# Relative attention on one core: two masked queries and the first products moved ahead, diagonals waited for block by block

## What is computed

```python
qx, kx, vx = split_head(x @ Wq.T), split_head(x @ Wk.T), split_head(x @ Wv.T)
ex = rel_embed[ns].reshape(n, NH, HD).transpose(1, 0, 2)
srel = srel_skew(jnp.einsum('bhnd,hmd->bhnm', qx, ex))
qk = (jnp.einsum('bhnd,bhmd->bhnm', qx, kx) + srel) * inv_dim
atten = jax.nn.softmax(qk - mask, axis=-1)
out = jnp.einsum('bhnm,bhmd->bhnd', atten, vx).transpose(0, 2, 1, 3).reshape(b, n, d)
return out @ Wp.T + bp
```

## Time and profile before

| | |
|---|---|
| median of three runs | 3797.18 us (3792.64 to 3798.52) |
| the profiled execution | 3799.16 us, of which the span of instructions 3797.1 us |
| PE busy | 3561.5 us, 94% |
| PEld, DVE, ACT, POOL busy | 63%, 60%, 46%, 22% |
| granted clock of TensorE, mean | 0.992 |

### The profile page before, as it was taken

How to read it: one execution, slowest core, us unless ns; L and a number is a source line. 1 busy time by engine, 2 the same in 40 slices (tenths; PEclk the granted TensorE clock), 3 DMA queues, 4 the chain that set the end, 5 groups by cost and what they waited for, 6 DMA issues and landing times.

```text
span 3797.1 us, 78536 instructions
## 1 busy us (share of the span) xinstructions
PE 3561.5 (94%) x31023; PEld 2402.4 (63%) x31023; DVE 2288.1 (60%) x7482; ACT 1731.8 (46%) x3542; POOL 822.9 (22%) x1374
## 2 busy tenths in 40 slices
PE   6999999988999999998899999998889999999888
PEld 3666667666565667766556556776665656677665
DVE  4546455677554655567755554567776555456766
ACT  2425333466442523356644252335565335233556
POOL 3202023411210302332021030333302112033330
PEclk8999999999999999999999999999999999999999
DMA  3000000000000000000000000000000000000000
GB/s 89 2 1 2 1 1 1 2 2 2 13 1 1 2 1 1 1 2 2 1 13 1 1 2 1 1 1 2 2 7 8 1 1 1 1 1 1 2 2 9
DMA packets 27032, 17.47 MB, mean 5 GB/s; under 512 B 9425, under 2 KB 26274, under 8 KB 26658
## 3 DMA queue, kind: packets, MB, share of 16 engines
q1 hardware_dynamic: 26658, 12.32, 1.2%
HBM read 10.22 MB, written 2.10 MB: 3 GB/s over the span
## 4 chain that ended last, share of the span: by engine, by line
PE 69%; DVE 11%; POOL 7%; ACT 6%; issue 5%; SPq 1%; DVEq 0%; another core or an unknown queue 0%; POOLq 0%
PE banks L1252 9%; PE banks L1219 8%; PE banks L1214 8%; PE banks L1064 5%; PE banks L1103 5%; POOL work L563 5%; PE banks L1118 4%; PE banks L1043 3%; PE banks L1306 3%; PE banks L1538 3%; ACT work L887 2%; ACT work L881 2%; PE banks L1373 2%; PE banks L1551 2%; DVE work L2034 2%
## 5 line engine op out<-in xcount | busy, mean ns | idle before, releaser
L1723 DVE CUSTOM_DVE_ANT_0 work<-banks,mask_row 128x512 f32<-128x512 f32 (+3 forms) x1024 | 433.9, 486 | 276.1 <-PE banks L1064 276.0
L718 ACT ACTIVATE work<-banks 128x512 f32<-128x512 f32 x352 | 209.3, 597 | 654.1 <-PE banks L1214 638.9
L1814 DVE TENSOR_TENSOR work<-work,banks 128x512 f32<-128x512 f32 x352 | 242.0, 688 | 426.5 <-PE banks L1219 404.6
L519 POOL TENSOR_TENSOR rstd<-rstd,half 128x4 f32<-128x4 f32 x65 | 65.6, 1009 | 1933.9 <-DVE rstd L1647 1933.9
L741 ACT ACTIVATE work<-banks 128x384 f32<-128x384 f32 (+1 forms) x768 | 358.8, 534 | 255.2 <-PE banks L1103 254.7
L1103 PE MATMUL banks<-work 32*128 32x512 f32 (+3 forms) x2048 | 443.8, 464 | 6.5 <-DVE work L1723 3.9
L1252 PEld LDWEIGHTS banks<-wd,work 128*128 128x128 f32 (+2 forms) x4096 | 355.0, 189 | 135.3 <-issue 131.4
L1064 PE MATMUL banks<-work 32*128 32x384 f32 (+3 forms) x2048 | 406.1, 457 | 11.9 <-ACT work L727 6.4
L1252 PE MATMUL banks<-wd,work 128*128 128x128 f32 (+2 forms) x4096 | 365.8, 278 | 0.0
L530 POOL TENSOR_SCALAR_AFFINE_SELECT work<-work 128x128 f32<-128x128 f32 (+1 forms) x768 | 253.4, 333 | 460.8 <-ACT work L741 437.5
L1103 PEld LDWEIGHTS banks<-work 32*128 32x128 f32 x2048 | 243.0, 183 | 77.2 <-ACT work L741 39.4
(11 more groups left out here) (320 smaller groups left out, 6596.6 us busy)
## 6 DMA issues: line engine op xcount, KB each, us to landing
x_a<-in_L_attn_a_x_dram SPq DMA_DIRECT2D x5, 256.0 KB, 2.8
x_b<-in_L_attn_a_x_dram SPq DMA_DIRECT2D x4, 256.0 KB, 3.0
wg<-in_L_ffn_Wg_dram SPq DMA_DIRECT2D x2, 512.0 KB
wu<-in_L_ffn_Wu_dram SPq DMA_DIRECT2D x2, 512.0 KB
wd<-in_L_ffn_Wd_dram SPq DMA_DIRECT2D x16, 64.0 KB
out_dram<-x_a SPq DMA_DIRECT2D x4, 256.0 KB, 2.5
out_dram<-x_b SPq DMA_DIRECT2D x4, 256.0 KB, 2.6
wk_l<-in_L_attn_a_Wk_dram SPq DMA_DIRECT2D x1, 512.0 KB, 4.1
```

Of the source, the lines that this page charges most:

```text
L1723: m = eng.tensor_tensor_reduce(out=summed[:, k % 2, col:col + N], in0=bank(bk)[:, col:col + N], in1=mask_row[:, T - N:T], scale=1.0, scala ...
```

## The change

Five edits, all in the relative attention.

1. The float32 rest of q goes to the buffer of normalized rows (`xns`), that of k to the memory of the second masked-query buffer. The first masked-query buffer is free from the start of the call.
2. DVE's order is new: the rest of q, masked high part for c = 0, the rest of k, masked middle part for c = 0, low part of q, low part of k, values, then c = 1, then both copies of spread k. Before it was: both rests, both low parts, values, both masks of c = 0, the first copy of spread k, c = 1, the second copy.
3. POOL's masked part for c = 1 waits for DVE's two masks of c = 0 (`r_qm`) in place of the low parts.
4. PE runs group 0 of the products first; the wait for the values and the spread steps 0 and 1 come between groups 0 and 1.
5. DVE's wait for all 32 diagonal instructions is split over the first three adds: job 0 waits for 29, job 1 for 31, job 2 for all.

```diff
--- before.py
+++ after.py
@@ -206,8 +206,9 @@
         q_st, at = part(0, [H // 2, T], BF16)
         k_st, at = part(at, [H // 2, T], BF16)
         ring_at = at
-        res, at = part(ring_at, [2, T])
-        k_parts, at = part(at, [3, T], BF16)
+        k_parts, _ = part(ring_at + 2 * T, [3, T], BF16)
+        res_k, _ = part(ring_at + 2 * T + 3 * T // 2, [T])
+        at = ring_at + 2 * T + 3 * T // 2
         q_parts, at = part(ring_at + 3072, [3, T + 2], BF16)
         qk_part = lambda w, n: (q_parts[:, n, 1:T + 1], k_parts[:, n, :])[w]
 
@@ -546,8 +547,7 @@
                 if c % 2 == 0:
                     return
                 if c == 1:
-                    eng.wait_ge(r_shift, n + 1)
-                    eng.wait_ge(a_lo, 2 * n + 2)
+                    eng.wait_ge(r_qm, 12 * n + 2)
                 else:
                     eng.wait_ge(r_rel_ok, 2 * (P // 8) * n + 2 * (IC // 8) * (c - 1))
                 mask_q(eng, c, 1).then_inc(r_qmp, 1)
@@ -684,6 +684,10 @@
             eng.wait_ge(xn_T, norm_number(j) + 1)
             eng.activation(xnTs[j % 2][:, :], bank(bk), ACT.Copy).then_inc(xnT_ok, 1)
 
+        def rest(n, w):
+
+            return (xns[n][:, :, :].rearrange("p t d -> p (t d)"), res_k)[w]
+
         def act_parts(eng, n, scale):
             eng.wait_ge(a_proj, 3 * n + 1)
             eng.activation(qk_part(0, 0), bank(0), ACT.Copy, scale=scale).then_inc(a_hi, 1)
@@ -691,7 +695,7 @@
             eng.activation(qk_part(1, 0), bank(1), ACT.Copy).then_inc(a_hi, 1)
             for w in range(2):
                 eng.wait_ge(a_res, 2 * n + w + 1)
-                eng.activation(qk_part(w, 1), res[:, w, :], ACT.Copy).then_inc(a_mid, 1)
+                eng.activation(qk_part(w, 1), rest(n, w), ACT.Copy).then_inc(a_mid, 1)
 
         def act_stack(eng, n, w, at):
 
@@ -1469,10 +1473,11 @@
             pe_project(eng, n, w)
             fill(eng, 3, 9)
             eng.wait_ge(a_res, 2 * n + 2)
-            eng.wait_ge(a_v, 4 + n + 1)
-            pe_spread(eng, n, 0)
-            pe_spread(eng, n, 1)
             for i in range(P // 8):
+                if i == 1:
+                    eng.wait_ge(a_v, 4 + n + 1)
+                    pe_spread(eng, n, 0)
+                    pe_spread(eng, n, 1)
                 for par in range(2):
                     k = 2 * i + par
                     if i >= 2:
@@ -1666,21 +1671,6 @@
                 eng.tensor_copy(values[:, :, :, 0:HD], bank(bk).rearrange("p (t h d) -> p t h d", t=NT, h=H))\
                    .then_inc(a_v, 1)
 
-            def parts_of_qk(n, scale):
-                for w in range(2):
-                    eng.wait_ge(a_hi, 2 * n + w + 1)
-                    eng.scalar_tensor_tensor(out=res[:, w, :], in0=bank(w), scalar=(scale, 1.0)[w],
-                                             in1=qk_part(w, 0), op0=ALU.mult,
-                                             op1=ALU.subtract).then_inc(a_res, 1)
-                eng.memset(q_parts[:, 0:2, 0:1], 0.0).then_inc(r_shift, 1)
-                for w in range(2):
-                    eng.wait_ge(a_res, 2 * n + w + 1)
-                    eng.wait_ge(a_mid, 2 * n + w + 1)
-                    eng.tensor_tensor(qk_part(w, 2), res[:, w, :], qk_part(w, 1),
-                                      ALU.subtract).then_inc(a_lo, 1)
-                eng.wait_ge(a_proj, 3 * n + 3)
-                copy_values(2)
-
             def stack_k(n, at):
                 i = spread_job(1, at)
                 eng.wait_ge(a_spread, H * n + i + 1)
@@ -1996,21 +1986,39 @@
                 add(n + 1)
 
             def rel(n):
-                parts_of_qk(n, float(HD) ** -0.5)
+                def first_rest(w):
+                    eng.wait_ge(a_hi, 2 * n + w + 1)
+                    eng.scalar_tensor_tensor(out=rest(n, w), in0=bank(w), scalar=(float(HD) ** -0.5, 1.0)[w],
+                                             in1=qk_part(w, 0), op0=ALU.mult,
+                                             op1=ALU.subtract).then_inc(a_res, 1)
+
+                def last_part(w):
+                    eng.wait_ge(a_res, 2 * n + w + 1)
+                    eng.wait_ge(a_mid, 2 * n + w + 1)
+                    eng.tensor_tensor(qk_part(w, 2), rest(n, w), qk_part(w, 1),
+                                      ALU.subtract).then_inc(a_lo, 1)
 
                 def mask(c):
-                    if c == 0:
-                        eng.wait_ge(r_shift, n + 1)
-                        eng.wait_ge(a_lo, 2 * n + 2)
                     if c >= 2:
                         eng.wait_ge(r_rel_ok, 2 * (P // 8) * n + 2 * (IC // 8) * (c - 1))
                     mask_q(eng, c, 0).then_inc(r_qm, 1)
                     if c % 2 == 0:
                         mask_q(eng, c, 1).then_inc(r_qm, 1)
 
-                mask(0)
+                eng.memset(q_parts[:, 0:2, 0:1], 0.0).then_inc(r_shift, 1)
+                first_rest(0)
+                eng.wait_ge(r_shift, n + 1)
+                mask_q(eng, 0, 0).then_inc(r_qm, 1)
+                first_rest(1)
+                eng.wait_ge(a_mid, 2 * n + 1)
+                mask_q(eng, 0, 1).then_inc(r_qm, 1)
+                last_part(0)
+                last_part(1)
+                eng.wait_ge(a_proj, 3 * n + 3)
+                copy_values(2)
+                eng.wait_ge(a_lo, 2 * n + 2)
+                mask(1)
                 stack_k(n, 0)
-                mask(1)
                 stack_k(n, 1)
                 for i in range(P // 8):
                     eng.wait_ge(r_rel_ok, 2 * (P // 8) * n + 2 * i + 1)
@@ -2024,10 +2032,11 @@
                 eng.wait_ge(r_late, P // 8 * n + P // 8)
                 eng.wait_ge(r_odd, P // 8 * n + P // 8)
                 eng.wait_ge(r_even, P // 8 * n + P // 8)
-                eng.wait_ge(r_diag, 4 * (P // IC) * n + 4 * (P // IC))
 
                 def add(p, j):
                     eng.wait_ge(r_main, 3 * PAIRS * n + 3 * p + j + 1)
+                    if p == 0:
+                        eng.wait_ge(r_diag, 4 * (P // IC) * (n + 1) - (3, 1, 0)[j])
                     b = JOB_AT[j] // P
                     for r in range(2):
                         v = sc[:, 2 * p + r, b:b + JOB_N[j] // P, :].rearrange("p b i -> p (b i)")
```

## The result

The changed kernel takes 3808.73 us (median of nine runs, 3802.80 to 3812.39), the kernel before 3796.75 beside it (3787.22 to 3800.35). The ratio is 1.004, interval 1.0031 to 1.0049: slower, by 12 us by the medians, by 15 by the ratio, and by 12 to 19 by its interval. The forecast was 3809 and "slower".

A forecast was written before the change was run, and what follows sets the result against it. PE and POOL were taken as equally near the bound of the products, DVE as bounding the opening. +8.5 us without the clock and +3.4 for clock falls gave +11.9 on 3797.18, about 3809.0 us; range 3791 to 3816.

The forecast's parts named there:

- The second low part: DVE's opening: the low part of k stands still beside POOL's mask, near 2.5 us in place of 0.69.
- the values are not held up: Rival, opening: DVE isn't blocked in the low parts, or keeps its turn for both; sum -6.2 us, 3791; chance 0.14.
- The turns: Opening: DVE and POOL alternate one instruction each: low part of q, POOL's mask, low part of k.
- PE and DVE in the opening: Opening: PE's group 1 is 1.09 us late, DVE's copy of group 0 is 1.47 us late.
- Lateness of the first clearing: POOL's diagonals start behind DVE's late copy of group 0, 1.47 us later than before.
- Carrying over: POOL has no pause, so its 1.47 us reaches its mask for c = 7 and the last diagonal whole.
- POOL makes up its part: Rival: only PE's 1.09 us is left at the products' end; +5.4 us, 3802.6; chance 0.12.
- Edit 5: End of the stage: job 1, behind ten fillers, gains 0.59 us in first calls, 0.23 in second; 3.3 us in all.
- The sum without the clock: Relative attention: +0.88 us in each first call, +1.24 in each second, four of each: +8.5 us.
- The clock: PE's 2.25 us opening pause makes the clock fall in two calls, 1.7 us each: +3.4 us.
- The share of one in four: Share of PE's opening pauses followed by a clock fall, from four of sixteen earlier pauses: two calls, +3.4 us.
- The clock falls in most calls: Rival: PE's longer opening pause lowers the clock in most calls; up to +22.1 us, 3819; chance 0.12.

The follow-up runs named there:

- Experiment 2: Changed kernel with POOL's first mask waiting for both low parts of q and k again: 3785.41 us against 3794.51 for the kernel before, ratio 0.9973.
- experiment 1: Kernel before with only the split wait for the diagonals added: 3789.83 us against 3794.51, ratio 0.9993.
- experiment 5: Changed kernel with the wait for the values and both spread steps ahead of group 0 again: 3824.87 us, ratio 1.0081 against the kernel before.
- experiment 4: The changed kernel measured again, unaltered, against the kernel before: 3806.91 us against 3793.61, ratio 1.0031.
- The filled pause: Changed kernel with nine fillers more in PE's pause between group 0 and the spreading, run twice: ratios 1.0022 and 1.0037 against the kernel before.
- experiments 8 and 10: 8: changed kernel, DVE copying values between the low parts, ratio 0.9969; 10: also copying group 0 before the low part of k, ten fillers, ratio 0.9971.

## Why the prediction was right

**The second low part.** Predicted: issued 4.11 us after the rest of q, standing still until POOL's mask is through, 2.5 us. Measured 4.07 and 2.52. Experiment 2 takes away POOL's mask alone, and the part is 0.68 again and the kernel faster: that POOL's mask is what holds it up is shown, not argued. The rival "the values are not held up" is refuted, but its arithmetic was good. It said -6.2, and experiment 2, which makes its condition true, moved job 1 by -7.1.

**The turns.** The order low part of q, POOL, low part of k was inferred from the earlier trace rows, and came so in all eight calls.

**PE and DVE in the opening.** Spreading at 7.34, group 1 at 9.94, group 0 copied at 11.12 were the forecast, from the rest of q; measured 7.25, 9.86 and 11.05. Lateness of the first clearing: 1.47 forecast, 1.40 measured.

**Carrying over.** "POOL makes up its part" is refuted: last clearing +1.43, first +1.40. PE stood 0.53 before the groups of c = 7.

**Edit 5.** Forecast 0.59 and 0.23, in all 3.3 us; measured alone (experiment 1) 0.66 and 0.31, 3.9 us. The fillers cap it. The add itself was forecast 1.4 us earlier and came 0.93 earlier; nothing hung on that, for the cap decides.

**The sum without the clock**: 8.5 forecast, 7.6 measured by the anchors. Each term was right in sign and within 0.1 us a call.

**The clock.** PE's idle was forecast at 2.25 us and measured at 1.99, because group 0 takes 1.56 to its end and not the 1.40 from start to start. I had put two falls at 1.7 us each, 3.4. Two traces of the changed kernel show none and four in eight openings, so two on average, at 1.21 to 1.68, 2.9 us a launch. The share of one in four, borrowed from shorter pauses, was met, but on two traces that is luck as much as reasoning. The share itself was read from sixteen pauses of 1.46 and 1.49 us; the same trace has six more, of 1.24 to 1.56 us, with no fall behind any, which makes it 4 of 22. "The clock falls in most calls" didn't happen here. It did in experiment 5, with a pause nearly twice as long.

**What stays open.** 7.6 and 2.9 make 10.5. The two comparisons say 15 (12 to 19) and 12 (7 to 16), so up to some 5 us have no place in the opening, and that 3809 and 3808.73 agree so closely is luck. The clock falls elsewhere too. From one turn's second call to the next turn's first the same instructions took 811.2 to 817.5 us within the trace of before. From the first call to the second, two turns of the first trace of the changed kernel took 126.1 and 126.4 us where two others took 124.7; but the trace of before has the same, 125.0 and 125.3 where two others took 123.9. Whether the change makes such falls more frequent isn't settled: over the whole span the mean granted clock was 0.994 and 0.995 in the two traces of the changed kernel and 0.992 in that of before, while in experiment 4 the mean over all executions was 0.9930 for the changed kernel and 0.9943 for the kernel before. The filled pause, which has no falls in its openings, wasn't clearly faster than the changed kernel, so the 2.9 us are read from traces and aren't confirmed by a time.

## What to carry to other kernels

When an instruction of POOL is released earlier, ask which DVE instructions with two inputs in SBUF then lie beside it, and who waits for the one that comes second; put copies out of PSUM there. With a low part of k blocked beside the same mask of POOL, the kernel was by the profile 7.6 us slower or 8.3 faster, by what stood behind the blocked one. Ending a wait that looks expensive gains only what the next instruction in line leaves: here the add came 0.93 us earlier, and behind ten fillers job 1 gained 0.66 and 0.31.

## What the runs showed of the hardware

Where both inputs of DVE's instruction lie in SBUF, DVE and POOL took turns by instruction: low part of q 0.69 us, POOL's mask 2.42, low part of k 2.52, in all eight calls. The Trainium skill (SBUF — State Buffer, "Who interferes with whom") says that a DVE instruction with at most one SBUF input, outside DVE's two-port modes, doesn't contend with GpSimd. The traces agree: the values took 0.68 to 0.69 us beside POOL's mask in experiments 8 and 10, while a low part took up to 2.52.

Not expected: how steeply the clock's falls came with the length of PE's pause. After 2.0 us (with 0.68 idle and 1.56 of products before it) the granted clock fell in 4 of 16 openings, all four in one of two traces; with the 2.0 us filled in 0 of 16; after 4.28 us in 8 of 8. In the nine other traces, whose openings have no pause over 1.2 us, it fell in 0 of 72. And the first add follows job 0 0.35 us later in the first call of a turn than in the second, in every kernel; no run explains it.
